# Row normalisation on GpSimd from mean and power, without VectorE's offset, in a cross-attention and feed-forward kernel

## The reference

```python
def _layernorm(x, axis=-1, eps=1e-05):
    m = jnp.mean(x, axis=axis, keepdims=True)
    v = jnp.var(x, axis=axis, keepdims=True)
    return (x - m) / jnp.sqrt(v + eps)

# cross attention over the 64 channels, 8 heads of 64 columns, all projections 64 x 64
x = x + xattn(_layernorm(x), ctx, ctx, Wq, bq, Wk, bk, Wv, bv, Wo, bo)
# feed-forward 512 -> 1792 -> 512; the weights are integers with zero points and scales for groups of 128
h = _layernorm(x)
gate = silu(h @ ((gate_w - gate_z) * gate_s))
up = h @ ((up_w - up_z) * up_s)
x = x + (gate * up) @ ((down_w - down_z) * down_s)
```

## Time and profile before

| | us |
|---|---|
| median of 3 runs | 435.77 (434.56 to 436.81) |
| profiled execution, its own time | 434.57 |
| its span | 432.8 |
| TensorE busy | 410.4 (95%) |
| VectorE busy | 330.4 (76%) |
| ScalarE busy | 330.5 (76%) |
| GpSimd busy | 265.8 (61%) |

### The profile page before, as it was taken

How to read it: one execution, slowest core, us unless ns; L and a number is a source line. 1 busy time by engine, 2 the same in 40 slices (tenths; PEclk the granted TensorE clock), 3 DMA queues, 4 the chain that set the end, 5 groups by cost and what they waited for, 6 DMA issues and landing times.

```text
span 432.8 us, 10751 instructions
## 1 busy us (share of the span) xinstructions
PE 410.4 (95%) x4228; PEld 317.9 (73%) x4228; DVE 330.4 (76%) x582; ACT 330.5 (76%) x540; POOL 265.8 (61%) x264
## 2 busy tenths in 40 slices
PE   7878988999988999999999999999999999999994
PEld 5655666777856777777777878677877888888872
DVE  4778666998878778788887777787887667667676
ACT  2438898897877788687778888687888998988970
POOL 3335797899588654665473954755566555555561
PEclk9899999999999999999999999999999999999999
DMA  7677746966742000002010000000000000001003
GB/s 255 190 230 259 279 147 226 300 204 209 241 121 69 2 11 16 26 2 76 12 39 26 2 0 27 27 2 26 26 27 0 2 1 9 17 24 50 1 1 97
DMA packets 26792, 35.44 MB, mean 82 GB/s; under 512 B 1870, under 2 KB 18422, under 8 KB 26742
## 3 DMA queue, kind: packets, MB, share of 16 engines
q1 hardware_dynamic: 26434, 34.71, 24.5%
q10 hardware_dynamic: 244, 0.05, 0.1%
q0 software_dynamic: 64, 0.00, 0.0%
HBM read 30.56 MB, written 4.19 MB: 80 GB/s over the span
## 4 chain that ended last, share of the span: by engine, by line
PE 73%; DVE 9%; issue 6%; POOL 6%; ACT 4%; DMA 1%; POOLq 0%; SPq 0%; DVEq 0%; ACTq 0%
PE banks L764 20%; PE banks L766 19%; PE banks L777 10%; PE banks L778 9%; PE banks L663 4%; DVE yT L1039 2%; PE banks L703 2%; ACT banks L555 2%; PE banks L692 2%; PE banks L673 2%; PE banks L681 2%; POOL t_sb L416 1%; DVE st L925 1%; PE banks L722 1%; DVE qkT L943 1%
## 5 line engine op out<-in xcount | busy, mean ns | idle before, releaser
L555 ACT ACTIVATE banks<-banks,ratio 128x512 f32<-128x512 f32 x336 | 207.8, 664 | 34.9 <-PE banks L766 25.4
L1039 DVE SCALAR_TENSOR_TENSOR yT<-banks,sd,yT 128x512 f32<-128x512 f32 x208 | 154.1, 746 | 48.8 <-PE banks L778 48.1
L764 PE MATMUL banks<-xT,wgu 128*128 128x512 f32 x448 | 182.2, 407 | 5.2 <-DVE t_sb L1024 2.5
L766 PE MATMUL banks<-xT,wgu 128*128 128x512 f32 x448 | 175.1, 391 | 0.0
L416 POOL TENSOR_TENSOR t_sb<-t_sb,u_sb 128x512 f32<-128x512 f32 x56 | 72.7, 1298 | 63.1 <-DVE t_sb L1024 63.0
L764 PEld LDWEIGHTS banks<-xT,wgu 128*128 128x128 f32 x448 | 84.1, 188 | 27.6 <-issue 3.7
L766 PEld LDWEIGHTS banks<-xT,wgu 128*128 128x128 f32 x448 | 84.3, 188 | 15.2
L777 PE MATMUL banks<-hr,wd 128*128 128x512 f32 x224 | 89.3, 399 | 4.2 <-DVE yT L1039 2.3
L778 PE MATMUL banks<-hr,wd 128*128 128x512 f32 x224 | 87.5, 390 | 0.0
L429 POOL TENSOR_TENSOR hr<-t_sb,hr 128x512 fp32r<-128x512 f32 x56 | 73.1, 1305 | 5.1 <-ACT hr L577 0.7
L777 PEld LDWEIGHTS banks<-hr,wd 128*128 128x128 f32 x224 | 42.0, 188 | 19.3 <-DVE yT L1039 9.5
(11 more groups left out here) (93 smaller groups left out, 383.9 us busy)
## 6 DMA issues: line engine op xcount, KB each, us to landing
x_sb<-in_x SPq DMA_DIRECT2D x16, 256.0 KB, 5.2
out<-x_sb SPq DMA_DIRECT2D x16, 256.0 KB, 2.1
wgu_in<-in_L_ffn_gate_w SPq DMA_DIRECT2D x7, 512.0 KB, 5.7
z_in<-in_L_ffn_gate_z SPq DMA_DIRECT2D x7, 512.0 KB, 5.4
wgu_in<-in_L_ffn_up_w SPq DMA_DIRECT2D x7, 512.0 KB, 5.5
z_in<-in_L_ffn_up_z SPq DMA_DIRECT2D x7, 512.0 KB, 5.0
wd_in<-in_L_ffn_down_w SPq DMA_DIRECT2D x7, 512.0 KB, 5.3
z_in<-in_L_ffn_down_z SPq DMA_DIRECT2D x7, 512.0 KB, 4.6
```

Source lines behind the costliest of these rows:

```text
L555: act.activation(banks[:, bank, :], banks[:, bank, :], ACT.Copy, scale=ratio[:, m, g, it:it + 1]).then_inc(done[n % 2], 1)
L764: pe.matmul(banks[:, bank, :], w, xT[:, c % 2, 0, g, :], start=g == 0, stop=False, skip_group_check=True)
L766: pe.matmul(banks[:, bank, :], w, xT[:, c % 2, 1, g, :], start=False, stop=True, skip_group_check=True).then_inc(full[n % 2], 1)
L1039: dve.scalar_tensor_tensor(y, bank, sd[:, it, b:b + 1], y, ALU.mult, ALU.add).then_inc(s_free, 1)
```

## The change

In the main loop the step "shift" is gone from VectorE, for both normalisations. norm1 and norm2 on GpSimd now compute (x - mean) * rs in one instruction, from VectorE's mv and GpSimd's own rs, and wait for rs instead of for nm. The tables lose the entry for shift; all other entries keep their places. The opening still makes nm for ScalarE.

```diff
-    norm1_at = [{} for _ in range(4)]
-    norm2_at = [{} for _ in range(5)]
-    x_after = norm2_at[4]
+    norm1_at = [{} for _ in range(3)]
+    norm2_at = [{} for _ in range(4)]
+    x_after = norm2_at[3]
...
-        for j, at in enumerate(((0, 1, 2, 3), (5, 6, 7, 8), (21, 22, 23, 24), (29, 30, 31, 32)) if c == 0 else
+        for j, at in enumerate(((0, 1, 3), (5, 6, 8), (21, 22, 24), (29, 30, 32)) if c == 0 else
...
             def norm1(t):
-                pool.wait_ge(s_nm[0], t + 1)
+                pool.wait_ge(s_rs[0], t + 1)
                 pool.wait_ge(s_bQK, t - 1)
-                pool.tensor_scalar(xn[:, t % 2, :], x_sb[:, t, :], rs[:, 0, t:t + 1], nm[:, 0, t:t + 1],
-                                   ALU.mult, ALU.add).then_inc(s_xnp, 1)
+                pool.tensor_scalar(xn[:, t % 2, :], x_sb[:, t, :], mv[:, 0, t, 0:1], rs[:, 0, t:t + 1],
+                                   ALU.subtract, ALU.mult).then_inc(s_xnp, 1)
 
             def norm2(t):
-                pool.wait_ge(s_nm[1], t + 1)
+                pool.wait_ge(s_rs[1], t + 1)
                 pool.wait_ge(s_full, slot["X", t - 2] + 1)
-                pool.tensor_scalar(xn2[:, t % 2, :], x_sb[:, t, :], rs[:, 1, t:t + 1], nm[:, 1, t:t + 1],
-                                   ALU.mult, ALU.add).then_inc(s_xn2p, 1)
+                pool.tensor_scalar(xn2[:, t % 2, :], x_sb[:, t, :], mv[:, 1, t, 0:1], rs[:, 1, t:t + 1],
+                                   ALU.subtract, ALU.mult).then_inc(s_xn2p, 1)
...
-                if q in norm2_at[3]:
-                    norm2(norm2_at[3][q])
-                if q in norm1_at[3]:
-                    norm1(norm1_at[3][q])
+                if q in norm2_at[2]:
+                    norm2(norm2_at[2][q])
+                if q in norm1_at[2]:
+                    norm1(norm1_at[2][q])
...
                     stats(1, norm2_at[0][q])
-                if q in norm2_at[2]:
-                    shift(1, norm2_at[2][q])
                 if q in norm1_at[0]:
                     stats(0, norm1_at[0][q])
-                if q in norm1_at[2]:
-                    shift(0, norm1_at[2][q])
```

More of the change, by code:

```diff
@@ L70, in xattn_ffn @@
                 burst_after[q0 + q] = (kind, t0 + j)
-        for j, at in enumerate(((0, 1, 2, 3), (5, 6, 7, 8), (21, 22, 23, 24), (29, 30, 31, 32)) if c == 0 else
-                               ((-5, -4, -3, -2), (5, 6, 7, 8), (13, 14, 15, 16), (27, 28, 29, 30))):
+        for j, at in enumerate(((0, 1, 3), (5, 6, 8), (21, 22, 24), (29, 30, 32)) if c == 0 else
+                               ((-5, -4, -2), (5, 6, 8), (13, 14, 16), (27, 28, 30))):
             if t0 + 1 + j < NT:
@@ L78, in xattn_ffn @@
                     table[PER * c + q] = t0 + 1 + j
-        for j, at in enumerate(((21, 22, 23, 24, 33), (32, 33, 34, 36, 44), (43, 44, 45, 46, 48), (46, 48, 48, 49, 51))
-                               if c == 0 else
-                               ((17, 20, 21, 22, 25), (28, 29, 30, 32, 35), (39, 40, 41, 44, 46), (42, 44, 45, 46, 49))):
+        for j, at in enumerate(((21, 22, 24, 33), (32, 33, 36, 44), (43, 44, 46, 48), (46, 48, 49, 51)) if c == 0 else
+                               ((17, 20, 22, 25), (28, 29, 32, 35), (39, 40, 44, 46), (42, 44, 46, 49))):
             for table, q in zip(norm2_at, at):
```

## The result

| | before | after |
|---|---|---|
| median of 6 runs | 435.92 (434.56 to 436.95) | 440.3 (439.24 to 441.97) |
| span of the profiled execution | 432.8 | 439.0 |

The change makes the kernel slower: the ratio is 1.011, 95% interval 1.0084 to 1.0136, 4.4 us between the medians. I had forecast 435.5 and a range up to 437.0.

What follows compares the result with a forecast made beforehand. TensorE, busy 95% of the span, was taken as fullest. -0.12 - 0.08 = -0.2 us against the median 435.77 gave 435.6; a tenth for earlier products made it 435.5 us, range 433.0 to 437.0.

Steps and rivals of the forecast that it cites:

- the price of the new form: GpSimd's 23 normalisations: 802 ns each, ends -3.8 and 11.4 us of GpSimd time, 0 us on the path.
- The costly form: Rival: the subtracting normalisation on GpSimd takes up to 1298 ns, about 1 us slower, 436.6 us; chance 0.10.
- +1 us at the high end: Path cost of longer GpSimd normalisations: value 0, at most a tenth of 11.4 us, for the crowded first 102 us.
- Nobody on TensorE waits for a normalised row: TensorE's waits: it waits for VectorE's gated product and GpSimd's hr (2.5 and 1.6 us), never for a normalised row.
- The removed offsets: VectorE, 23 offsets of 0.12 us: only those at 129.76 and 144.49 us gain, 0.12 and 0.08 us.
- The first rival: All VectorE time was on the path: 2.8 us, 3.8 with earlier products, giving 432.0 to 433.0 us; chance 0.12.
- The wait: GpSimd's second normalisation waits 15.6 us for the offset; most becomes a wait for VectorE's gated product, value 0.
- The lock: GpSimd and VectorE block each other near 126 to 128 us; VectorE gets the turn, priced at 0.
- the second rival: GpSimd keeps the turn at 127.96 us, holding VectorE's zero-point subtraction: 0.6 us slower, 436.3 us; chance 0.08.
- the earlier product: GpSimd's product after the freed wait starts about 0.3 us earlier at five places: value 0, at the fast end 1 us.

Runs made afterwards that it cites:

- e2_mult_add: Changed kernel with mult, add in place of subtract, mult on the same operands (not the normalisation): 435.33 us, ratio 1.0008.
- e12_three_spared: Kernel before with (x - mean) * rs in 20 of 23 normalisations, not norm2 of tile 4 or norm1 of tiles 6 and 7: 435.58 us, ratio 1.0006.
- e4_late_only: Kernel before with the change only for tiles 9 to 15 of norm1 and 8 to 15 of norm2 (15 of 23): 435.03 us, ratio 0.999.
- e1_form_alone: Kernel before, its offsets and waits kept, with (x - mean) * rs in all 23 normalisations: 439.92 us, ratio 1.0108.
- e7_pool_offset: Changed kernel, but GpSimd makes the offset itself in a 128x1 instruction and multiplies and adds as before: 437.33 us, ratio 1.003.
- e5_one_dear: Kernel before with (x - mean) * rs for norm2 of tile 4 alone; one run, read from its trace: hidden block 7 0.88 us late.
- e6_swap: Changed kernel with norm1 emitted ahead of norm2 where both stand at one place: 440.29 us, ratio 1.0109.
- e3_forms: Changed kernel with nine pairs of operations spread over its 23 normalisations, most not normalising; one run to read durations, no total time given.
- e11_kept_busy: Kernel before with (x - mean) * rs for norm2 of tile 4 and norm1 of tile 7, plus three idle-filling matmuls before tile 7's projection: 437.61 us, ratio 1.0058.

## Why the prediction was wrong

**The step that failed** is the price of the new form: "I take 802, since it too is one tensor with two scalars for each row", with the upper end at "23 x 0.50 = 11.4 us of GpSimd time". It measured 2.08 to 2.12 us, above the end that I called high: 23 x 1.3 = 30 us of GpSimd time. The bound was built from neighbours of the same size (cast, product of two tensors), as if the number of inputs set the price; the pair of operations set it (e2_mult_add, same inputs, 0.82 us), and no row of before had a subtraction of this kind. The costly form was among the rivals, with "up to 1298 ns" and a chance of 0.10, so the case was seen and its size cut off.

**The second error followed**: "+1 us at the high end (a tenth of the 11.4, for the crowded first 102 us)". Spread evenly, a tenth of 30 us would be 3 us, near the result by luck. What decides is place: three instructions bring the loss, twenty bring none that the times show (e12_three_spared, e4_late_only). "Nobody on TensorE waits for a normalised row" was true and was read as slack without measuring it. At 89.63 the row was ready 0.60 us ahead of the burst that reads it; two instructions 1.3 us longer eat that and 2 us more. I should have gone through the 23 places for how late each may be, as I did for the 23 offsets.

**The rest, by its steps:**
- The removed offsets: right in place, and within 0.1 us in size. Blocks 12 and 14 come earlier by 0.19 and 0.13 us in the changed kernel (0.22 and 0.15 in e2_mult_add), where I had 0.12 and 0.08; no other block gains by more than 0.1. Block 14's gain, 0.09 to 0.15, shows in all seven kernels in which VectorE doesn't make that offset there, and in none of the six others that keep it (0.02 at most). Block 12's is less clean: 0.08 to 0.10 of it shows in three kernels that keep the offset (e1_form_alone, e4_late_only, e12_three_spared). The first rival (3.8 us) is refuted by e2_mult_add, which has everything that it needs. A slip beside it: GpSimd is busy for 81.50 of the 102 us, 79.9%, not over 80%.
- The wait: it went (15.6 to 0.3 us) and brought nothing, as said. That it would turn into a wait of L415 for L1023 was not seen, since the dear form filled it.
- The lock, at the place that I priced: VectorE got the turn, as said, in the changed kernel too (134.05 against 133.50). In e2_mult_add it waits behind GpSimd's subtraction, ends 0.55 us behind it (127.62 against 127.07), and the normalisation is drawn out:

```profile
124.67 2.40 POOL L408 TENSOR_TENSOR wd_in<-wd_in,z_in 128x1024 int32<-128x1024 int32 x1
125.59 2.03 DVE L996 TENSOR_TENSOR wgu<-wgu_in,z_in 128x512 fp32r<-128x512 int32 x1
...
127.05 1.21 POOL L401 TENSOR_SCALAR xn<-x_sb,mv,rs 128x512 f32<-128x512 f32 x1
...
131.66 1.28 POOL L428 TENSOR_TENSOR hr<-t_sb,hr 128x512 fp32r<-128x512 f32 x1
131.79 1.71 DVE L996 TENSOR_TENSOR wd<-wd_in,z_in 128x512 fp32r<-128x512 int32 x1
...
134.21 0.50 PE L776 MATMUL banks<-hr,wd 128*128 128x512 f32 x1 [0.70 <-DVE yT L1038]
```

- But the last three rows show the second rival, GpSimd's turn, one block on. In the kernel before the same two met so, VectorE first by 0.03 us:

```profile
132.81 0.68 DVE L997 TENSOR_TENSOR wd<-wd_in,z_in 128x512 fp32r<-128x512 int32 x1
132.84 1.81 POOL L429 TENSOR_TENSOR hr<-t_sb,hr 128x512 fp32r<-128x512 f32 x1
```

With the normalisation earlier, GpSimd's L428 is first by 0.13 us, VectorE's subtraction is the one held (1.71), and TensorE waits 0.70 us. That is block 13's +0.94 in e2_mult_add and +0.93 in the changed kernel (GpSimd at 138.10, VectorE at 138.23): more than the offsets' whole gain. I had valued the earlier product "0, at the fast end 1 us" and not looked at what it would collide with. The Trainium skill, "SBUF — State Buffer", section "Who interferes with whom", says that the order of issue decides who blocks; 0.16 us in the order moved the block from one engine to the other here, so the traces agree.
- The clock stood in no part of the prediction. The steps less their waits at block 7 price its fall there: 3.62 - 2.10 = 1.5 and 4.62 - 3.03 = 1.6 us where the clock fell; 3.23 - 3.17, 1.87 - 1.81 and 0.88 - 0.80, all under 0.1, where it did not (e1_form_alone, e7_pool_offset, e5_one_dear).

The sum for the changed kernel's profile: 1.25 (block 4) + 2.1 (wait) + 1.5 (clock) + 0.93 - 0.19 - 0.13 = 5.5, and 0.7 of block 1 that is not the change's, is 6.2. That the form is the cause, and that three places carry it or nearly all of it, is shown by runs; that the clock's fall adds 1.5 us at block 7 is shown in single executions. What stays open: whether the clock falls behind such a wait in a given execution (it fell behind 2.10 and 3.03 us, and in e6_swap behind 1.83 and 2.02, not behind 3.17 and 1.81), and so how the 4.4 us of the medians divide.

## What to carry to other kernels

An instruction form that no row of the trace shows has no upper bound from its neighbours of the same size: measure the pair of operations by itself before rewriting a formula, and try the equal formula with another pair (x plus the negated mean cost 0.81 us where x minus the mean cost 2.1). When an instruction may get longer, ask at each of its places how long before its reader it ends; two that stand back to back ahead of one reader count together. An instruction that comes earlier can lose too: look at which operation of the other engine it now precedes by a tenth of a microsecond.

## What the runs showed of the hardware

- GpSimd, one tensor of 128x512 in 32 bits with scalars for each row: 0.76 to 0.78 us for mult with add in either order or mult with mult; 2.08 to 2.10 for the three pairs with a subtract and for add with add; 1.57 to 1.59 for one operation alone (e3_forms, without the two drawn out). The Trainium skill, "GPSIMD Engine Reference", section "Engine selection", calls GpSimd roughly at line rate with one input; the rows here differ by a factor of 2.7 with one input, and the measurement decides.
- The dear form holds VectorE up only in its first part, and no longer than the cheap one does. A subtraction of VectorE with two inputs in SBUF, 0.68 us undisturbed, took 0.68 when it began 1.27 us into a dear normalisation (91.36 in 90.09 to 92.17, shown above) and 0.84 when it began 0.46 us into one (92.62 in 92.16 to 94.23), where it ended 1.30 us behind that one's start. Beside a cheap one it ended 1.31 us behind the start (90.17 against 88.86), which is 0.54 behind its end. The reading that the prediction weighed, a lock held for an instruction's whole length, thus fits the cheap form here and not the dear one. The dear form itself can be drawn out (2.46 to 2.60 us).
- Waits of similar length were or weren't followed by a fall of TensorE's clock, as listed above. In the profiled execution with matmuls in the gap (e11_kept_busy) it stayed up.
